# Attention stack: rows of both parities as 128 partitions in one step, by groups of heads; the constant rows written to scratch once, early

## The reference, cut to what matters

```python
kqv = layernorm(x) @ W_kqv.T            # B=2, T=1024, 16 heads of D=8
q = rms_norm(rope(q), q_norm_w); k = rms_norm(rope(k), k_norm_w)
scores = einsum('bhtd,bhsd->bhts', q, k) / sqrt(8)
att = softmax(where(causal, -inf, scores))
y = einsum('bhts,bhsd->bhtd', att, v)
out = y.reshape(B, T, 128) @ W_proj.T
```

## Time and profile before

| | us |
|---|---|
| median of 3 runs (1013.46 to 1014.35) | 1013.97 |
| the profiled execution | 1014.45 |
| its span, first to last record | 1012.7 |
| PE busy | 689.1 (68%) |
| DVE busy | 537.7 (53%) |
| ACT busy | 394.1 (39%) |
| POOL busy | 346.0 (34%) |

### The profile page before, as it was taken

One profiled execution on the slowest core, in us unless ns is written; L12 is line 12 of the kernel. 1 busy time (PEld: TensorE's weight loads), 2 busy tenths in 40 slices (PEclk: granted clock), 3 DMA queues, 4 the chain that ended last, 5 costly groups with the idle time before them and its releaser, 6 DMA issues.

```text
span 1012.7 us, 13109 instructions
## 1 busy us (share of the span) xinstructions
PE 689.1 (68%) x4600; PEld 501.6 (50%) x4606; DVE 537.7 (53%) x1503; ACT 394.1 (39%) x697; POOL 346.0 (34%) x376
## 2 busy tenths in 40 slices
PE   2069797429999972098984489898538419889880
PEld 1056685112222231075874378787527417778780
DVE  6986657930111138976756344444358663545442
ACT  3053322429999962063412133333233103333330
POOL 2172212202232313180201346565330043556543
PEclk9569898758999996599995599999868558999996
DMA  6000000499200000000001445556310063555544
GB/s 252 0 1 1 1 1 15 135 171 167 31 2 1 2 1 1 0 1 1 1 5 41 157 134 177 176 175 152 94 44 1 0 191 92 155 167 177 172 102 135
DMA packets 33885, 79.26 MB, mean 78 GB/s; under 512 B 5192, under 2 KB 19784, under 8 KB 33304
## 3 DMA queue, kind: packets, MB, share of 16 engines
q1 hardware_dynamic: 27928, 66.21, 23.2%
q0 software_dynamic: 5888, 12.16, 5.3%
HBM read 62.47 MB, written 15.50 MB: 77 GB/s over the span
## 4 chain that ended last, share of the span: by engine, by line
PE 48%; DVE 21%; DMA 9%; issue 9%; ACT 6%; POOL 3%; SPq 2%; another core or an unknown queue 0%; DVEq 0%; ACTq 0%; POOLq 0%
PE ps L1661 12%; PE ps L1672 7%; DMA arena<-xs,wq 4%; ACT arena L1267 4%; PE ps L1582 4%; PE ps L1360 3%; PE ps L1485 3%; DMA arena<-scr_k 2%; DVE arena L608 2%; DVE arena L613 2%; PE ps L1565 2%; PE ps L1329 2%; PE ps L1456 2%; PE ps L1430 2%; PE ps L1467 2%
## 5 line engine op out<-in xcount | busy, mean ns | idle before, releaser
L1661 PE MATMUL ps<-arena 128*128 128x256 f32 x736 | 178.3, 398 | 26.0 <-issue 24.6
L1661 PEld LDWEIGHTS ps<-arena 128*128 128x128 f32 x736 | 143.2, 200 | 49.8 <-issue 30.0
L838 DVE SCALAR_TENSOR_TENSOR arena<-ps,arena 128x256 f32<-128x256 f32 x184 | 88.9, 483 | 140.6 <-ACT arena L1298 75.6
L1298 ACT ACTIVATE arena<-ps,arena 128x256 f32<-128x256 f32 x184 | 87.3, 474 | 184.1 <-PE ps L1661 93.2
L1267 ACT ACTIVATE arena<-ps 128x512 f32<-128x512 f32 (+3 forms) x192 | 138.3, 826 | 16.4 <-PE ps L1565 15.1
L511 POOL DMA_INDIRECT yd<-arena,wq x92 | 91.0, 989 | 120.7 <-DVE arena L858 99.0
L484 POOL DMA_INDIRECT arena<-xs,wq x92 | 89.7, 975 | 42.0 <-issue 26.5
L1672 PE MATMUL ps<-arena 128*128 128x128 f32 x736 | 91.1, 278 | 2.2 <-DVE arena L858 2.2
L1672 PEld LDWEIGHTS ps<-arena 128*128 128x128 f32 x736 | 87.1, 194 | 2.7 <-issue 2.6
L473 POOL TENSOR_SCALAR_AFFINE_SELECT arena<-arena 128x512 f32<-128x512 f32 x64 | 40.8, 637 | 128.0 <-ACT arena L1267 128.0
L1582 PE MATMUL ps<-arena 128*32 128x512 f32 (+3 forms) x768 | 82.7, 503 | 2.4 <-DVE arena L1063 1.6
(11 more groups left out here) (243 smaller groups left out, 1250.4 us busy)
## 6 DMA issues: line engine op xcount, KB each, us to landing
arena<-in_wall SPq DMA_DIRECT2D x46, 836.0 KB
arena<-yd SPq DMA_DIRECT2D x8, 512.0 KB, 5.4
arena<-scr_q SPq DMA_DIRECT2D x4, 768.0 KB, 14.5
arena<-scr_k SPq DMA_DIRECT2D x4, 768.0 KB, 19.9
xs<-Xn SPq DMA_DIRECT2D x8, 260.0 KB, 5.0
scr_q<-arena SPq DMA_DIRECT2D x4, 384.0 KB, 6.8
scr_k<-arena SPq DMA_DIRECT2D x4, 384.0 KB, 4.6
arena<-xs,wq POOLq DMA_INDIRECT x92
```

Of the source, the lines that this page charges most:

```text
L838: nc.vector.scalar_tensor_tensor(out=hT[:, j % 2, f, :], in0=ps[:, 3 + k % 3, 0:TS], scalar=raw[:, slot, EW_BB + f:EW_BB + f + 1], in1=sl[ ...
L1298: nc.scalar.activation(sl[:, k % 3, :], ps[:, k % 3, 0:TS], ACT.Silu, bias=raw[:, slot, EW_BA + f:EW_BA + f + 1]).then_inc(sem("silu", i), 1)
L1661: ins = mm(ps[:, bank, 0:TS], raw[:, slot, w + P * f:w + P * (f + 1)], xTt[:, j % 2, :], start=True, stop=True)
```

## The change

Slots become 8 "lanes" per dimension (`LANES` = 8, of which the last two are the constant ones): the scratch tensors get the shape (128, 8, 2048), and the contraction of a score goes from 51 to 64 rows, so that `(r d m)`, parity, dimension and lane, are 128 partitions of one DMA. The stack of a batch is loaded in 8 DMAs, for each group of heads Q and K: 128 partitions x 2 pairs of heads x 1024 tokens, 512 KB each. Batch 0 has one semaphore per group of heads, and PE waits for a group's two loads just before its first score; batch 1 has one semaphore for all 8. The constant lanes go into the scratch tensors once, at the start of the program, by four DMAs of 512 KB that SP issues after the input loads, behind a wait for the tile `zeroone`; the 8 constant-row DMAs of the sublayer and PE's wait for them go. SP waits for these four just before it issues the stack loads. The preload of the Exp table moves from behind ACT's last part to just behind the root of batch 1. The semaphores `x_in` and `yf_in` are merged into one name, with the counts set to match. The branch of the row maximum is adapted; it is not taken.

```diff
--- before.py
+++ after.py
@@ -44,9 +44,10 @@
 
 SLOT_A, SLOT_B = (0, 0, 0, 1, 1, 2), (0, 1, 2, 0, 1, 0)
 NSLOT = len(SLOT_A)
+LANES = 8
+MAX_LANE = NSLOT
 SAME = ((0, 3), (3, 2), (5, 1))
-R_MAX = NSLOT * AD
-R_ALL = R_MAX + 3
+R_ALL = LANES * AD
 
 E_, F_ = 8, 512
 FT = F_ // P
@@ -150,7 +151,7 @@
         bound = sb("bound", [P, 16])
         warm = sb("warm", [P, 4])
         flag = sb("flag", [1, 1], mybir.dt.int32)
-        onezero = sb("onezero", [3, 2, T], BF16)
+        zeroone = sb("zeroone", [P, 2, T], BF16)
         nullk = sb("nullk", [P, 2, G * ET])
         nulltok = sb("nulltok", [P, D])
         ARENA = 34 * 1024 + 256
@@ -234,7 +235,7 @@
         rc = v["rc"].rearrange("p (i t h) -> p i t h", i=2, t=4)
         msp = v["msp"].bitcast(BF16).rearrange("p (c t) -> p c t", c=3)
         mrest = v["mrest"]
-        scr = [nc.dram_tensor(n, (D, NSLOT, B * T), BF16, kind="Internal").ap() for n in ("scr_q", "scr_k")]
+        scr = [nc.dram_tensor(n, (D, LANES, B * T), BF16, kind="Internal").ap() for n in ("scr_q", "scr_k")]
         scr_m = nc.dram_tensor("scr_m", (3, AH, B * T), BF16, kind="Internal").ap()
 
 
@@ -298,13 +299,15 @@
         ENDS = [n + 1 for n, x in enumerate(STEPS) if x[4]]
         UNIT = [sum(x[4] for x in STEPS[:n]) for n in range(len(STEPS) + 1)]
 
+        stacked = lambda b, hg: "stack_1" if b else f"stack_0{hg}"
+
         block = ctx.enter_context(nc.Block())
 
 
         @block.sync
         def _(sp):
             for t in range(4):
-                sp.dma_start(X[:, 4 * t:4 * t + 4, :], a["x"][:, 4 * t:4 * t + 4, :]).then_inc(sem(f"x_in{t}"), 16)
+                sp.dma_start(X[:, 4 * t:4 * t + 4, :], a["x"][:, 4 * t:4 * t + 4, :]).then_inc(sem(f"chunk_in{t}"), 16)
             sp.dma_start(consts[:, :], a["consts"]).then_inc(sem("const_in"), 16)
             sp.dma_start(wr[:, :], a["wr"]).then_inc(sem("wr_in"), 16)
             for n in ("wq", "wk", "wv", "wout", "nullk", "nulltok"):
@@ -314,17 +317,15 @@
             sp.dma_start(moec[:, :], a["moec"]).then_inc(sem("smallw_in"), 16)
             sp.dma_start(linc[:, :], a["linc"]).then_inc(sem("smallw_in"), 16)
             sp.dma_start(attw[:, :], a["attw"]).then_inc(sem("smallw_in"), 16)
+            sp.wait_ge(sem("zeroone"), 1)
+            for k in range(2):
+                for b in range(B):
+                    sp.dma_start(scr[k][:, NSLOT:LANES, T * b:T * (b + 1)],
+                                 zeroone[:, k:k + 1, :].broadcast_to([P, LANES - NSLOT, T])).then_inc(sem("lanes"), 16)
 
             def attn(i):
                 if i:
                     sp.wait_ge(sem("x_done"), i)
-                sp.wait_ge(sem("onezero"), 1)
-                for b in range(B):
-                    for par in range(2):
-                        for k, dst in ((0, Ks), (1, Qs)):
-                            sp.dma_start(dst[64 * par + R_MAX:64 * par + R_ALL, :, T * b:T * (b + 1)],
-                                         onezero[:, k, :].unsqueeze(1).broadcast_to([3, AH // 2, T])
-                                         ).then_inc(sem("maxrow", i), 16)
                 for b in range(B):
                     ts = slice(T * b, T * (b + 1))
                     for n in range(4 * b, 4 * b + 4):
@@ -336,11 +337,12 @@
                                          ).then_inc(sem(f"scr_{b}", i), 16)
                     sp.wait_ge(*at(f"scr_{b}", i, 16 * 4 * len(SAME)))
 
-                    for par in range(2):
+                    sp.wait_ge(sem("lanes"), 16 * 2 * B)
+                    for hg in range(NHG):
+                        pair = slice(HG // 2 * hg, HG // 2 * (hg + 1))
                         for k, dst in enumerate((Qs, Ks)):
-                            src = scr[k].rearrange("(h r d) m t -> r (d m) h t", r=2, d=AD)
-                            sp.dma_start(dst[64 * par:64 * par + R_MAX, :, ts], src[par, :, :, ts]
-                                         ).then_inc(sem(f"stack_{b}", i), 16)
+                            src = scr[k].rearrange("(h r d) m t -> (r d m) h t", r=2, d=AD)
+                            sp.dma_start(dst[:, pair, ts], src[:, pair, ts]).then_inc(sem(stacked(b, hg), i), 16)
 
                 sp.wait_ge(sem("flag"), 1)
                 unbounded = sp.value_load(flag[0:1, 0:1], min_val=0, max_val=1)
...
@@ -1076,8 +1078,8 @@
             def setup():
 
                 dve.wait_ge(sem("const_in"), 16)
-                nc.vector.memset(onezero[:, 0, :], 1.0)
-                nc.vector.memset(onezero[:, 1, :], 0.0).then_inc(sem("onezero"), 1)
+                nc.vector.memset(zeroone[:, 0, :], 0.0)
+                nc.vector.memset(zeroone[:, 1, :], 1.0).then_inc(sem("zeroone"), 1)
                 nc.vector.tensor_copy(identb[:, :], ident).then_inc(sem("identb"), 1)
                 nc.vector.tensor_copy(upper[:, :], consts[:, C_UPPER:C_UPPER + P])
                 nc.vector.memset(ones[:, :], 1.0)
...
@@ -1223,6 +1225,8 @@
                     act.wait_ge(*at("ss", i, TB * (b + 1)))
                     of_b = slice(TB * b, TB * (b + 1))
                     nc.scalar.activation(rr[:, of_b, :], ss[:, of_b, :], ACT.Sqrt, scale=1.0 / AD).then_inc(sem("rms", i), 1)
+                    if b == B - 1:
+                        preload(ACT.Exp)
 
                 def part(p_, n):
 
@@ -1255,7 +1259,6 @@
                     if n < 7:
                         part(0, n + 1)
                     part(1, n)
-                preload(ACT.Exp)
                 act.wait_ge(*at("split", i, 2 * NC))
                 for s_, (b, hg, qc, kt, last_) in enumerate(STEPS):
                     n = HALF - P * max(0, kt - 4 * qc)
@@ -1520,10 +1523,16 @@
                 for n in range(4, 8):
                     kq_transposes(n)
                 pe.wait_ge(*at("split", i, 2 * NC))
-                pe.wait_ge(*at("maxrow", i, 16 * 8))
+
+                def stack_landed(b, hg):
+                    if b == 0:
+                        pe.wait_ge(sem(stacked(b, hg), i), 16 * 2)
+                    elif hg == 0:
+                        pe.wait_ge(sem(stacked(b, hg), i), 16 * 2 * NHG)
 
                 def first_scores(b):
-                    pe.wait_ge(*at(f"stack_{b}", i, 16 * 4))
+                    for hg in range(NHG):
+                        stack_landed(b, hg)
                     for n in range(TB * AH):
                         qt, h = n // AH, n % AH
                         m = TB * AH * b + n
@@ -1533,8 +1542,8 @@
                         keys = P * (qt + 1)
                         for k0 in range(0, keys, HALF):
                             kn = min(HALF, keys - k0)
-                            ins = mm(ps[:, 2 * (n % 3) + k0 // HALF, 0:kn], Qs[lo:lo + R_MAX, h // 2, q0:q0 + P],
-                                     Ks[lo:lo + R_MAX, h // 2, T * b + k0:T * b + k0 + kn], start=True, stop=True)
+                            ins = mm(ps[:, 2 * (n % 3) + k0 // HALF, 0:kn], Qs[lo:lo + R_ALL, h // 2, q0:q0 + P],
+                                     Ks[lo:lo + R_ALL, h // 2, T * b + k0:T * b + k0 + kn], start=True, stop=True)
                         ins.then_inc(sem("s1", i), 1)
                     pe.wait_ge(*at("mx", i, b + 1))
                     for t in range(TB):
@@ -1552,8 +1561,8 @@
 
                 def scores(s_):
                     b, hg, qc, kt, last_ = STEPS[s_]
-                    if s_ in (0, len(STEPS) // 2):
-                        pe.wait_ge(*at(f"stack_{b}", i, 16 * 4))
+                    if s_ == 0 or STEPS[s_ - 1][0:2] != (b, hg):
+                        stack_landed(b, hg)
                     q0 = P * max(0, kt - 4 * qc)
                     n = HALF - q0
                     for u in range(2):
```

More of the change, by code:

```diff
@@ L355, in attn @@
                             src = scr_m.rearrange("c (h r) t -> r c h t", r=2)
-                            sp.dma_start(Qs[64 * par + R_MAX:64 * par + R_ALL, :, ts], src[par, :, :, ts]
+                            sp.dma_start(Qs[64 * par + MAX_LANE:64 * par + MAX_LANE + 2 * LANES + 1:LANES, :, ts], src[par, :, :, ts]
                                          ).then_inc(sem("max_in", i), 16)
@@ L381, in moe @@
                                  yd[HALF * 2 * c:HALF * 2 * (c + 1), :].rearrange("(t p k) d -> p t (k d)", p=P, k=2)
-                                 ).then_inc(sem(f"yf_in{c}"), 16)
+                                 ).then_inc(sem(f"chunk_in{c}"), 16)
             for i, kind in enumerate(kinds):
@@ L515, in moe @@
                     ts = slice(4 * c, 4 * c + 4)
-                    pool.wait_ge(sem(f"yf_in{c}"), 16 * (before + 1))
+                    pool.wait_ge(sem(f"chunk_in{c}"), 16 * (before + 2))
                     nc.gpsimd.tensor_tensor(yf[:, ts, 0, :], yf[:, ts, 0, :], yf[:, ts, 1, :], ALU.add
@@ L1097, in _ @@
             for c in range(NC):
-                dve.wait_ge(sem(f"x_in{c}"), 16)
+                dve.wait_ge(sem(f"chunk_in{c}"), 16)
                 row_stats(c, 0)
```

## The result

| | before | changed |
|---|---|---|
| median of 7 runs, us | 1013.46 | 1005.64 |
| lowest to highest | 1009.07 to 1017.07 | 1001.18 to 1009.85 |
| the profiled execution | 1014.45 | 1005.23 |
| its span | 1012.7 | 1003.5 |

The ratio is 0.9927, 95% interval 0.9904 to 0.9950: 7.4 us faster, between 5 and 10 (the medians differ by 7.8). I had forecast 999.8 (14.2 less) in a range up to 1003.5. The change does what it says, and half of the expected gain isn't there.

What follows compares the result with a forecast made beforehand. The prediction took the stack load of K before the attention's first score as the bound. Terms -14.4 (loads) and +0.2 (constant lanes) sum to -14.2: 1014.45 becomes 1000.25, 999.8 as median; range 998.6 to 1003.5.

Steps and rivals of the forecast that it cites:

- What bounded the kernel before: Before the attention's first score: PE idle 18.6 us, released by the stack load of K, a 24.40 us link.
- So from 211.54 to 226.01 nothing but DMA ran: Between DVE's last part of `split` and PE's first score, only the stack loads were said to be running.
- Loads by groups of heads, and PE's waits: At the first score: only 2 loads of 512 KB needed, landing before `split` ends; start 211.6 instead of 226.01, gain 14.4 us.
- The rate: Stack loads into 128 partitions: taken as 303 GB/s, the rate of the `x` loads, instead of 128 to 135.
- Rival 1: Stack loads: their rate doesn't rise, being set per packet or by DRAM reads; 0 to 1.5 us lost, 1000 to 1001.5; chance 0.06.
- Rival 2: Scratch writes before the loads slow at the new pitch; loss 3.4 (to 8.9) us, likeliest 1003.5; chance 0.07.
- Rival 3: Program start: constant-lane writes delay `attw` by up to 2.7 us and shift all behind it, 1002; chance 0.04.
- 0.2 in my sum: Program start: cost in us taken for writing the constant lanes while the input loads end; bounds 0 and 2.7.
- Rival 4: Mid-attention: batch 1's stack comes late if reads collapse; slower than before from 107 GB/s, 1028.6 at 90; chance 0.04.
- Steps, 64 rows, clock, preload: Attention steps, 64-row matmuls, TensorE's clock and the moved Exp preload: each taken as 0; clock could give 0.8 at most.
- The direction: Whole kernel: forecast and rivals 1 to 3 all faster by more than 0.2% (2 us), together 0.95.

Runs made afterwards that it cites:

- narrow loads: Changed kernel with each stack load cut by parity into 64 partitions, 16 DMAs of 256 KB per batch; 211 GB/s instead of 385, gap from `split` to first score 10.32 us.
- all eight awaited: Changed kernel, branch in its old place, with PE waiting for all eight loads of batch 0 before the first score; gap 7.62 us beside 7.35 and 7.37.
- short jump: Changed kernel with the body of PE's row-maximum branch cut to one wait, branch kept in place; gap from `split` to first score 1.85 us.

## Why the prediction was wrong, by its own steps

- *What bounded the kernel before*: right. The load was the last to arrive, and without the branch the first score still waited for it.
- *"So from 211.54 to 226.01 nothing but DMA ran"*: this is the sentence that failed, and with it the step *Loads by groups of heads, and PE's waits*, "the next late thing is `split` ... and the first score starts at 211.54 + 0.06 = 211.6". I asked which wait ends next and looked for it among the records. A register read and a branch leave none. They stood in the kernel's code between the wait and the first score, they lay under the load, and they were worth 7.3 us once it was gone. The term was sized 14.4 and measured 7.11. The 0.06 itself is right: with read and branch away the gap is 0.06.
- *The rate*: right where the sum used it. The loads ran at 275 GB/s in their first 4 us and at 385 after that, beside the 303 I took from the first stretch of `x`; the pair landed by 206.9 (205.8 and 206.8 forecast), all eight by 215.8 (215.1 forecast). What I had not thought of is that the rate also sets how late the instructions come (10.3 us of gap at 211 GB/s, 7.35 at 385). Of the 14.47 us between `split` and the first score 7.35 stayed; that it was not more I owe to the rate, by a way that is not in the prediction.
- *Rival 1* (rate set per packet): refuted by the narrow loads. Its price was wrong too: "0 to 1.5 lost". With narrow loads the gap is 3.0 larger than with wide ones, and at the old rate the packet would have left a gain of 1.1 to 2.7 us (the estimate above), not the 12.7 to 14.2 of that rival. And *"the gain comes from the grouping, not from the rate"* is the wrong way round as the kernel stands: all eight awaited costs 0.3.
- *Rival 2* (writes slower at the new pitch): 263 GB/s beside 264, no effect of a pitch of 32 KB instead of 24. The reads, with rows 4 KB apart, dimensions 32 and pairs of heads 512, reached 385 GB/s. The Trainium skill's warning of large powers of two ("DMA: Bandwidth & Descriptors", "Latency and other measured facts") begins at 512 KiB from one partition to the next, and nothing here has that pitch, so the runs neither confirm nor deny it.
- *Rival 3* (the start): no delay that stands out of the scatter, the wait for `attw` ending at 20.30 to 21.27 beside 20.76. The 0.2 in my sum is not shown.
- *Rival 4* (batch 1 late): loads issued from 225.18, the last at 229.43 and landed by 240.6 (241.7 forecast), no wait in the steps.
- *Steps, 64 rows, clock, preload*: the attention from first score to the next sublayer's first DMA took 153.90 before and 153.91 after. Together the four terms were 0 as taken; one by one they were not measured.
- *The direction*: faster by more than 0.2% had 0.95 and came true, for the reason given; only the size was off, by the term above.
- No rival had a hidden stall of PE's own program. The Trainium skill has the rule ("Runtime: NRT & Kernel Launch", section "Instruction fetch mechanics"): a taken branch whose target lies outside the instructions held forces a DMA fetch before execution goes on. By it the jump should have been a rival of mine. The short jump and the long one agree with it, 1.85 and 7.35 us; the page gives no price.

## What to carry to other kernels

When a wait is removed, read the program and not only the trace between that wait and the first instruction that counts: register reads, branches and far jumps leave no record, and a long wait covers them. A DMA view cut into short stretches still dates the packet of a far jump. Put a branch over a large block, and the read that feeds it, where its engine is idle anyway, even if a few instructions then stand in both arms. Load over all 128 partitions in one DMA where the loads bound something; finer semaphores pay only if nothing else stands between the wait and the work.

## What the runs showed of the hardware that I had not expected

- A jump over a large block cost TensorE 3.0 us with empty DMA engines, 5.7 with wide loads and writes running and 8.7 with narrow ones (gaps of 4.63, 7.35 and 10.32, less the 1.64 without it; the 7.35 came again as 7.37 and 7.30, the others are of one profile each). Its 16 KB instruction packet is counted on the same 16 DMA engines as the data and starts later the slower the data move: 1.7 to 2.2 us after `split` on empty engines, 4.5 to 5.1 at 380 to 385 GB/s, 6.7 to 7.7 at 211 to 215, 9.5 to 10.5 at 128 to 136.
- A jump over a block of one wait cost 0.2 us (one profile; three gaps of kernels with equal PE code lie within 0.07).
- Reading one flag from SBUF into a register of TensorE, with the wait ahead of it, was worth 1.6 us between two dependent steps (1.64 against 0.06).
- Loads from DRAM in 2 KB packets ran at 128, 211 and 385 GB/s into 48, 64 and 128 partitions per DMA. The rate does not grow in proportion from 48 to 64; why was not tried.
